# 16-head cross-attention over four layers: score products in two 64-row strips, f32 projections of a host-transposed context, one ring of PSUM banks, and an unread f32 product in steps without other products

## What is computed

```python
def attention(q, k, v):                       # 16 heads of 8 features
    s = einsum("bshd,bkhd->bhsk", q, k) / sqrt(8)
    return einsum("bhsk,bkhd->bshd", softmax(s), v)

xn, cn = rmsnorm(x, gq), rmsnorm(ctx, gkv)                       # layer 0
x = xn + attention(xn @ wq.T, cn @ wk.T, cn @ wv.T) @ wo.T + bo
o = attention(x @ Wq.T + bq, ctx @ Wk.T + bk, ctx @ Wv.T + bv, masked)   # layer 1
x = layernorm(x + o @ Wo.T + bo)
a = layernorm(x + attention(..., causal over 100 x 1444))        # layer 2
x = a + gelu(a @ W1.T + b1) @ W2.T + b2
x = layernorm(x + attention(x @ Wq + bq, ctx @ Wk + bk, ctx @ Wv + bv))  # layer 3
```

## Time and profile before

| | |
|---|---|
| Median of 3 runs | 1241.33 us (1240.63 to 1242.63) |
| The profiled execution | 1242.44 us |
| Its span, first to last instruction | 1240.6 us |
| Mean granted clock of TensorE | 0.959 of 2.4 GHz |
| Busy: TensorE (PE), VectorE (DVE), ScalarE (ACT), GpSimd (POOL) | 1059.6, 857.3, 825.3, 372.6 us |
| Chain that ended last, by engine | PE 58%, DVE 16%, issue 10%, ACT 10%, SP's DMA queue 3% |
| Chain, by line | sexp L700 15%, acc L719 14%, smax L664 12%, mx L1096 7%, probs L965 5% |

### The profile page before, as it was taken

One profiled execution on the slowest core, in us unless ns is written; L12 is line 12 of the kernel. 1 busy time (PEld: TensorE's weight loads), 2 busy tenths in 40 slices (PEclk: granted clock), 3 DMA queues, 4 the chain that ended last, 5 costly groups with the idle time before them and its releaser, 6 DMA issues.

```text
span 1240.6 us, 30123 instructions
## 1 busy us (share of the span) xinstructions
PE 1059.6 (85%) x9938; PEld 638.9 (51%) x9938; DVE 857.3 (69%) x1757; ACT 825.3 (67%) x1788; POOL 372.6 (30%) x339
## 2 busy tenths in 40 slices
PE   1469888888998999988998889998999989998886
PEld 0245445445555555655555555565556556565442
DVE  5678678578766766875876657576777858777650
ACT  1237756667776777776777676657677766767565
POOL 6744433344411311330231413232242413323000
PEclk9979999899999999998999999799999999999898
DMA  7212212212221221221232120202021121201100
GB/s 187 62 37 58 61 27 58 58 30 60 65 58 33 73 74 32 72 79 38 58 77 52 39 71 21 55 24 58 22 62 35 48 61 28 61 24 31 35 3 4
DMA packets 57587, 62.92 MB, mean 51 GB/s; under 512 B 16826, under 2 KB 50906, under 8 KB 57302
## 3 DMA queue, kind: packets, MB, share of 16 engines
q1 hardware_dynamic: 57430, 60.89, 19.0%
HBM read 23.63 MB, written 0.41 MB: 19 GB/s over the span
## 4 chain that ended last, share of the span: by engine, by line
PE 58%; DVE 16%; issue 10%; ACT 10%; SPq 3%; DMA 1%; POOL 1%; DVEq 0%; ACTq 0%; POOLq 0%
PE sexp L700 15%; PE acc L719 14%; PE smax L664 12%; DVE mx L1096 7%; ACT probs L965 5%; PE shared L616 3%; PE shared L604 3%; SPq L403 2%; DVE mneg L1102 2%; PE shared L593 2%; PE shared L784 2%; PE smax L676 1%; DVE qs L1083 1%; PE shared L626 1%; SPq L469 1%
## 5 line engine op out<-in xcount | busy, mean ns | idle before, releaser
L965 ACT ACTIVATE probs<-sexp 120x400 f32<-120x400 f32 (+1 forms) x1152 | 558.9, 511 | 237.9 <-PE sexp L700 226.6
L1096 DVE TENSOR_TENSOR mx<-smax,mx 120x400 f16<-120x400 f32 (+1 forms) x1056 | 557.2, 567 | 167.7 <-PE smax L664 161.4
L700 PE MATMUL sexp<-qexp,krep 97*120 97x400 f16 (+1 forms) x1152 | 403.8, 360 | 61.1 <-ACT probs L965 41.8
L664 PE MATMUL smax<-qmax,krep 96*120 96x400 f16 (+1 forms) x1152 | 367.3, 350 | 37.5 <-DVE mx L1096 29.1
L700 PEld LDWEIGHTS sexp<-qexp,krep 97*120 97x120 f16 (+1 forms) x1152 | 152.1, 136 | 216.7 <-ACT probs L965 144.6
L719 PE MATMUL acc<-probs,vx 120*18 120x200 f32 (+1 forms) x4608 | 262.1, 347 | 1.0 <-ACT probs L965 0.9
L664 PEld LDWEIGHTS smax<-qmax,krep 96*120 96x120 f16 (+1 forms) x1152 | 157.6, 138 | 92.6 <-DVE mx L1096 51.3
L488 POOL TENSOR_TENSOR ct<-ctf,ct 128x480 f16<-128x480 f32 (+1 forms) x72 | 82.8, 1151 | 346.2 <-ACT ct L902 346.2
L719 PEld LDWEIGHTS acc<-probs,vx 120*18 120x18 f32 (+1 forms) x4608 | 109.0, 99 | 114.8 <-issue 84.5
L1094 DVE CAST mx<-smax 121x400 f16<-121x400 f32 x96 | 51.3, 570 | 120.3 <-PE smax L664 120.2
L488 POOL TENSOR_TENSOR kp<-kf,kp 128x480 f16<-128x480 f32 (+1 forms) x72 | 79.2, 1106 | 114.6 <-ACT kp L916 114.6
(11 more groups left out here) (133 smaller groups left out, 994.0 us busy)
## 6 DMA issues: line engine op xcount, KB each, us to landing
nat<-in_ctx SPq DMA_DIRECT2D x24, 720.0 KB
krep<-kp SPq DMA_DIRECT2D x576, 30.0 KB, 1.9
krep<-kp SPq DMA_DIRECT2D x288, 30.2 KB, 1.9
qexp<-qmax SPq DMA_DIRECT2D x24, 300.0 KB, 3.4
maskexp<-maskmax SPq DMA_DIRECT2D x8, 281.2 KB, 3.4
anymask<-in_mask SPq DMA_DIRECT2D x1, 1128.1 KB, 6.7
mask<-in_mask SPq DMA_DIRECT2D x8, 141.0 KB
wq<-in_w_qkv SPq DMA_DIRECT2D x1, 768.0 KB
```

Of the source, the lines that this page charges most:

```text
L664: last = pe.matmul(ps, krep[0:PARTS, u.par, t, c0:c0 + r], qmax[:, u.par, t, :, :].rearrange("p h s -> p (h s)"), start=True, stop=not masks)
L700: last = pe.matmul(ps, krep[:, u.par, t, c0:c0 + r], qexp[:, u.par, t, :, :].rearrange("p h s -> p (h s)"), start=True, stop=not masks)
L965: act.activation(probs[0:r, j % PR, :], sexp[j % SR][0:r, 0:QW], ACT.Exp).then_inc(sem["probs_ready"], 1)
L1096: op = dve.tensor_tensor(dst, src, dst, ALU.max)
```

## The change

- **Strips.** The array's rows are used in two strips of 64. A strip holds 16 features (two heads) in 3 x 16 = 48 rows (`KROWS`), and for the exponentials a 49th row of ones. Tile `j` is now chunk `j // 4`, pair of quarters `j // 2 % 2`, strip `j % 2`, again 4 heads by 100 rows, made by two products of 200 columns in the same strip. `exp_product` and `max_product` alternate, and because the maxima are 13 tiles (`LEAD`) ahead, they are always in the other strip. Chunks but the last of each group load 128 columns of weights, the 7 or 8 last of which belong to the next chunk and are not read.
- **One query tile.** `qx`, a ring of three, serves both products; the copy to `qexp` is gone and the row of maxima is written into `qx` by two DMAs.
- **Maxima.** One in each step, 13 ahead: the unit n+1 from its tile 13 to its last, and from step 35 the unit n+2. `mx` is doubled.
- **Banks.** Three banks `sexp`, and one ring of four for the maxima and all other products, given out in the order of issue (`place`, `SLOT`). The accumulation is one step later.
- **Projections.** Keys, values and queries are single f32 products; the bias of the queries is a product of one row. The f16 weights and context are gone. The host passes the context transposed as well: layers 1 and 3 load `ctf` directly (`load_transposed`), layer 0 still loads by row, normalises and transposes. The keys are written to DRAM (`kept`, 3 DMAs) and read back in strips by 6 DMAs a group instead of 12.
- **Queries.** ScalarE copies the high part, VectorE makes high and low with one instruction; GpSimd spreads over 2 heads instead of 4.
- **Unread product.** `keep_clock`: in a step from the seventh on in which no other product stands, one f32 product of the 128 x 128 identity by 112 of its columns, into the columns 400 to 511 of the bank `acc`, which nothing reads.
- **Mask.** Its transposes read consecutive columns of `maskb`, where they read every twelfth.
- **No loops.** All 28 stages are written out; the two bodies are for the stages 6 to 15.

```diff
-PR, SR, MR = 10, 2, 3
-PARTS = 3 * 32
+PR, SR, RING = 10, 3, 4
+PARTS = 128
+STRIP = 64
+KROWS = 48
...
-VALUES_AT = [j // TOGETHER * TOGETHER + TOGETHER + 1 for j in range(NSTEP)]
-MAX_AT = [i * 39 // NSTEP for i in range(NSTEP)]
-MT_AT = 39
+VALUES_AT = [j // TOGETHER * TOGETHER + TOGETHER + SR - 1 for j in range(NSTEP)]
+LEAD = 13
...
+        def tile_of(j):
+
+            return j // T, j // 2 % 2, j % 2
+
+        def max_tile(s, j):
+
+            u, i = (s.top, j + LEAD) if j + LEAD < NSTEP else (s.prep, j + LEAD - NSTEP)
+            return (u, i) if u is not None else None
...
+            def load_transposed(u, before):
+
+                sp.wait_ge(*at("v_filled", before, 3))
+                sp.dma_start(ctf[:, u.par, :], ctxT_in[u.batch]).then_inc(sem["ctx_loaded"], 16)
...
+                for i in range(2):
                     for j, part in enumerate((0, 0, 1)):
-                        sp.dma_start(krep[32 * j:32 * j + 32, u.par, t, c0:c0 + n],
-                                     kp[32 * t:32 * t + 32, part, c0:c0 + n]).then_inc(sem[f"krep_in{g}"], 16)
...
+                        at_row = STRIP * i + 16 * j
+                        sp.dma_start(krep[at_row:at_row + 16, u.par, :, c0:c0 + n],
+                                     kept[u.par, :, part, c0:c0 + n].rearrange("(t i r) n -> i r t n", t=T, i=2)[i]
+                                     ).then_inc(sem[f"krep_in{g}"], 16)
...
-                for j, (w, c) in enumerate(((0, 0), (0, 1), (1, 0))):
-                    last = pe.matmul(ps[:, 0:n], wk16[:, w, u.L, :], ct[:, u.par, c, c0:c0 + n], start=(j == 0),
-                                     stop=(j == 2))
-                last.then_inc(sem["k_filled"], 1)
+                pe.matmul(ps[:, 0:n], wk[:, u.L, :], ctf[:, u.par, c0:c0 + n], start=True, stop=True
+                          ).then_inc(sem["k_filled"], 1)
...
+            def columns(c):
+
+                return ROWS[c] if c % 4 == 3 else 128
...
+                last = pe.matmul(bank(f"smax{j}", u)[0:n, 2 * S * a:2 * S * a + 2 * S],
+                                 krep[at_row:at_row + KROWS, u.par, 2 * tp + a, c0:c0 + n],
+                                 qx[at_row:at_row + KROWS, u.third, 2 * tp + a, :, :].rearrange("p f s -> p (f s)"),
+                                 start=(a == 0 or not masks), stop=not masks, skip_group_check=masks)
...
+            def keep_clock():
+
+                pe.matmul(acc[:, QW:512], ident[:, :], ident[:, 0:512 - QW], start=False, stop=True, skip_group_check=True)
+
             def stage(s, n, masks=False):
                 for j in range(NSTEP):
-                    if s.exp is not None:
-                        exp_scores(s.exp, j, masks and s.exp.L == 1)
-                    for i in range(NSTEP):
-                        if MAX_AT[i] == j and s.top is not None:
-                            max_scores(s.top, i, masks and s.top.L == 1)
+                    m = max_tile(s, j)
+                    for a in range(2):
+                        if s.exp is not None:
+                            exp_product(s.exp, j, a, masks and s.exp.L == 1)
+                        if m is not None:
+                            max_product(*m, a, masks and m[0].L == 1)
...
+                    if s.exp is not None and j >= VALUES_AT[0] and not other_products(s, n, j):
+                        keep_clock()
```

More of the change, by code:

```diff
@@ L670, in maxima @@
[L670 to L678 removed]
+                                 tile[0:r, c, :].unsqueeze(1).broadcast_to([r, HT, S]), start=False, stop=True,
```

716 lines of the change are left out of this document (349 added, 367 removed).

## The result

The changed kernel takes **1440.35 us** (median of 4, 1428.31 to 1445.05) where the kernel before takes 1241.98 us beside it (median of 4, 1240.63 to 1243.05): a ratio of 1.158, with an interval of 1.151 to 1.166. It is slower by 198 us; forecast were 1107 us and a range up to 1260. The profiled execution took 1445.05 us, 3.7 more than its span.

What follows compares the result with a forecast made beforehand. PE was taken as the bound, its standard-stage load rising from 34.0 to 38.0 us, with waits cut to 2 us. A start of 86 us, stages of about 40 and 48 us and the ending summed to 1107 us; range 1030 to 1260.

Steps and rivals of the forecast that it cites:

- The head: Start of the kernel, up to the first exponential: 86 us for 91.
- The 0.07 falls on each: PE's changes between 64 and 128 rows: 0.07 us each, the middle between bounds 0 and 0.14.
- rival (a): Each change of array shape on PE costs the full 0.14 us: 1165 us in all, chance 0.22.
- Scores 0.20 us: A step's four score products on PE, priced like packed accumulation pairs: 0.20 us, 9.6 us a stage for 16.6.
- The unread product: Added f32 product on PE, issued 588 times: 0.306 us each, 8.3 us in a standard stage.
- a gain in waits: PE's waits in a standard stage: 2 us left (3 with layer 2), where 7.1 and 8.8 stand now.
- Keys 0.80, values 0.90.: f32 projection groups on PE: keys 0.80 us for 0.63, values 0.90 us for 0.67.
- As much again for the bias: Query bias products on PE in layers 1 and 3: as much as the queries' 0.94 us.
- Rival (d): Half-height and unread products don't hold PE's clock: mean 0.83 gives 1280 us, break-even from 0.86 down; chance 0.08.
- Rival (c): The strips' score products do not overlap: four take 0.345 us, 167 us more, 1274 us in all; chance 0.10.
- Rival (b): Shape changes and unread products fall into PE's idle time, ACT and DVE decouple fully: 1040 us, chance 0.13.
- the last stage gets slower: Last stage, without maxima to pair with: 31 us on PE, slower than 30.5 by 1 to 2 us.

Runs made afterwards that it cites:

- a_bias128: Changed kernel with the queries' bias product on 128 rows (127 of them zero) instead of 1 row; 1377.24 us, 1.110 of the kernel before.
- a_few_o2: Changed kernel with 1 instead of 16 of layer 2's value products for each batch, leaving out 15 heads' outputs; 1343.05 us, 1.082 of the kernel before.
- b_keep: Kernel before with only the f32 unread product on 128 rows added, in steps without other products; 1282.95 us, ratio 1.033.
- a_keep64: Changed kernel with the f32 unread product on 64 rows instead of 128; 1278.95 us, 1.029 of the kernel before.
- a_keep_f16: Changed kernel with the unread product in f16 instead of f32, still on 128 rows; 1284.24 us, 1.034 of the kernel before.
- a_nokeep: Changed kernel without its 588 unread products; 1211.51 us, 0.976 of the kernel before.
- c_o_later: Changed kernel without unread products, bias on 128 rows, layer 2's value products moved to steps 44 and 45; 1174.25 us, 0.949 of the kernel before.
- a_lead12: Changed kernel with LEAD 12 instead of 13, so both score tiles of a step share one strip; 1907.35 us, 1.534 of the kernel before.
- c_both: Changed kernel with bias on 128 rows, layer 2's value products five steps later, 64-row unread products in the last two stages only; 1159.63 us, ratio 0.936.
- a_keep64_late: Changed kernel with bias on 128 rows, 64-row unread products only in steps 34 to 43 of stages 13 to 20; 1197.11 us, ratio 0.962.

## Why the prediction was wrong

The forecast was 1107 us, the profiled execution took 1445. The head came out right (86.3 us for 86). The six stages 0 to 5 took 298 for 240 us, stages 6 to 12 362 for 280, stages 13 to 20 548 for 385, the last three 139 for 106: with 1 us around them, all of the 338. Stages of each kind exist at a clock of 1.00: 46.3 us, 47.7 for 6 to 12 (46.3 of `a_bias128` and 1.4 for the bias), 57.3 with layer 2 (54.5 of `a_few_o2` and 2.8). With these, an estimate from stages of other kernels, about 140 us of the 338 are clock (18 in stage 0, 28 in stages 6 to 12, 89 in 13 to 20, some 5 in 21), and about 200 are work on PE. Even at full clock the changed kernel would be slower than the one before.

**"The 0.07 falls on each" (the price of a change of shape).** This step failed first. I took the middle between 0 and 0.14 us, because no row showed a change from half the rows. Measured, the unread product takes 0.41 us for a forecast of 0.306 and rival (a)'s 0.38; the same product in the kernel before takes 0.21. With the 0.18 us that stand behind the last score product (200 columns need 0.09), going out and in costs up to 0.09 + 0.20 = 0.29 us. The upper bound itself was wrong: the accumulations' 0.14 us was taken as the dearest case because it was the only one. The measured price is that of an f32 product: in f16 the same place takes 0.16 us, some 0.05 of it for 112 columns (an estimate from 0.09 for 200), so 0.11 us on the way out. That a change of height has one price whatever the product was wrong too. The Trainium skill (TensorEngine Tiling (Array Packing), Key Properties) has the rule that changing the mode drains TensorE, without a price. `b_keep` against the changed kernel (0.21 for 0.41 us) and `a_keep64` against both agree with it; `a_keep_f16` shows that it is not all. Rival (a), with a chance of 0.22, was right that changes of height cost, and still too cheap.

**"Scores 0.20 us" for four.** They take 0.27 us, 0.07 more and about 3 us a stage with the changes of shape. The rate inside was right: 90 ns from pair to pair. The error was to take a row of packed pairs, the accumulations, whose way out stands once behind 16 records, as the price of four records whose way out stands in every step. The unread product is what makes nearly every step have a way out: where two steps stand back to back in `a_nokeep`, 8 products take 0.48 us in the median of 179, and not twice 0.28.

**"The unread product"** as a whole was put at 8.3 us a stage and measured at 10.98, and over the kernel at 588 x 0.306 = 180 us and measured at 229 by its removal. The prediction had it as PE's dearest addition and then let a gain in waits pay for it. Waits did come out at nothing where 2 us were left: but 7 us of coupling cannot pay for 11 us of product. Without it a standard stage takes 38.2 to 38.5 us for 40.8, so the rest of the change alone gains some 2.4 us.

**"Keys 0.80, values 0.90."** Measured 1.01 and 1.07. 480 columns at 1.68 ns are 0.80 us and 8 records at 118 ns 0.94; the other 0.2 and 0.13 us fit the way out, since a 64-row product follows, but no run takes them apart. The context's transposes went from 0.42 to 0.56, the transposes of the output from 0.44 to 0.58, wo from 0.22 to 0.39: every excursion from the strips took longer, 2.5 us a stage in all. I had charged it 17 times, at a third of its price.

**"As much again for the bias".** It was put at 1.9 us with the queries, and is 3.1: 0.39 for each of eight products. That each of these changes between 1 row and 128 was not seen at all.

**Rival (d), the clock, with a chance of 0.08.** It happened: 0.858, near the 0.86 that it named as its limit. The reason against it, "PE has less idle time than now", was the step that failed. PE had next to none, and the clock fell, for the longest times behind work and not behind idle time. The trace of before held the counter-example, which the prediction did not use. This is its timeline at the start of the long fall in the stage whose clock is 0.89 in the earlier trace rows:

```profile
776.94 0.91 PE L784 MATMUL shared<-v,pT 100*100 100x9 f32 x8
777.70 0.57 PE L700 MATMUL sexp<-qexp,krep 97*120 97x400 f16 x1
```

PE goes from one product to the next, and at the score product of 777.70 (0.57 us for 0.33) it is at half speed, behind the same small products. Before, this happened in one of eight such stages at this step; in the changed kernel, whose scores are half as high, in all eight. That the height of the scores is what takes the margin away is argued, not shown: no run has the strips of before with the rest of the change. There is a rival that nothing tests. The change also regroups these products: before they stand in four groups of 8 records at steps 37 to 40 (774.13, 775.22, 776.94 and 778.07 us), with scores between, now in two of 16 at steps 39 and 40 (`AT2["o"] - 1 + t // 2` for `AT2["o"] - T + 1 + t`). Which of the two makes the fall regular is open. `a_few_o2`, `a_bias128` and `c_o_later` show which groups set off a fall.

**Rival (c)** is refuted by the start times and by `a_lead12`; the Trainium skill (TensorE: Matmul & The Clock Gate, Part 3) says that products in different row groups run at once, and the trace agrees (both strips' products start at 331.16 us). **Rival (b)**, that everything falls into idle time, did not happen: a standard stage has no idle time on PE left to fall into (46.15 of 46.20 us busy).

**What held.** The start; the accumulations, 0.805 us for 0.805; that DVE and ACT stay behind PE, at 30 to 32 us and 35 to 39 with layer 2; that neither the keys' way over DRAM nor the row of maxima makes a wait; that DVE's 4 us at the end of a stage go; that the last stage gets slower, though by 10 us and not by 1 to 2: its two score products a step, put at 0.173 us, take 0.29 with the way out, and 41 unread products 0.41 each. The range, up to 1260, would have taken in the unread product's true price alone or the clock's alone, not both.

## What to carry to other kernels

Where products of different height alternate on PE, count the changes and not only the columns: going from 64-row strips to 128 rows and back cost up to 0.29 us here around an f32 product that is itself 0.21, so filler and small products should have the height of what stands around them, or at least not be f32 (filler of 64 rows cost 67 us and filler of 128 rows in f16 73, where f32 filler of 128 rows cost 229; and a bias product on 128 rows cost less than one on a single row between products of 128). Read the clock's falls in the trace of before by what PE did just ahead of them, not by its idle time alone: groups of tiny products lowered the clock of a PE that was busy 95%. And when an edit adds work to the engine that bounds and takes waits away from it, the waits that it can take away are the ceiling of what it can pay for.

## What the runs showed of the hardware

- Two 64-row strips overlap in full: four products of 200 columns take 0.27 us in two strips and 0.45 us in one.
- Between 64-row score products an unread product of 112 columns takes 0.41 us in f32 on 128 rows and 0.16 us in f16 on 128 rows; the f32 one takes 0.21 us between score products of 96 and 97 rows.
- With the scores one after another in one strip, a PE busy 97% had a clock of 0.707; in two strips at once, 0.858.
- A fall of the clock that started behind layer 2's small products lasted 20.5 to 30.7 us in the changed kernel, though the usual work followed at once. At 1.2 GHz a step's scores took 0.45 us for 0.28 and the unread product 0.70 for 0.41, that is 1.6 to 1.7 times as long, not twice.
- With the 64-row unread product the clock was at 1.00 in the last two stages (`c_both`), and next to layer 2's small products it fell all the same (`a_keep64_late`). With the f16 one on 128 rows the last stage had 0.50.
